# An attention block's SP queue: the third part of q sent behind the first part of k

## What is computed

```python
q = x @ w_dq.T @ w_uq.T
kv = x @ w_dkv.T @ w_ukv.T
attn = softmax(q k^T * SCALE + causal mask);  out = (attn v) @ w_out.T
h = _layernorm(x) * (1 + ca) + sa;  x = x + ga * attention(h)
h = _layernorm(x) * (1 + cb) + sb;  x = x + gb * ffn(h)
```

## Time and profile before

| | |
|---|---|
| median of 3 runs | 596.92 us (595.57 to 600.63) |
| the profiled execution | 593.84 us, span 592.1 us, granted clock 0.951 |
| busy, share of the span | PE 87%, DVE 81%, ACT 62%, POOL 53% |
| chain that ended last, by engine | PE 49%, DVE 19%, DMA 10%, issue 9%, SP's queue 5% |
| largest DMA of the chain | qs<-parts_q, 8% |
| DMA issues of the stacks | 96 to qs (median 4.0 us to landing), 96 to ks (4.7 us) |

### The profile page before, as it was taken

How to read it: one execution, slowest core, us unless ns; L and a number is a source line. 1 busy time by engine, 2 the same in 40 slices (tenths; PEclk the granted TensorE clock), 3 DMA queues, 4 the chain that set the end, 5 groups by cost and what they waited for, 6 DMA issues and landing times.

```text
span 592.1 us, 14257 instructions
## 1 busy us (share of the span) xinstructions
PE 515.4 (87%) x4912; PEld 446.2 (75%) x4912; DVE 480.8 (81%) x949; ACT 366.5 (62%) x521; POOL 311.9 (53%) x300
## 2 busy tenths in 40 slices
PE   4534685989999999999999999999999999999974
PEld 4424463788888988888888888788988898888874
DVE  3538163779999899989898989999899999887573
ACT  1524464858585866667676858585766667676320
POOL 6235232455656665755646565656665665552441
PEclk9856598899999999999999999999999999999998
DMA  8835453262707080716244351708080615210100
GB/s 246 206 46 76 50 74 75 52 95 37 128 18 145 2 161 3 121 42 90 71 68 93 50 111 31 130 7 154 0 152 13 108 39 91 55 39 2 37 19 18
DMA packets 43802, 43.74 MB, mean 74 GB/s; under 512 B 5344, under 2 KB 40800, under 8 KB 43760
## 3 DMA queue, kind: packets, MB, share of 16 engines
q1 hardware_dynamic: 43760, 43.19, 39.1%
HBM read 13.39 MB, written 4.23 MB: 30 GB/s over the span
## 4 chain that ended last, share of the span: by engine, by line
PE 49%; DVE 19%; DMA 10%; issue 9%; SPq 5%; POOL 3%; ACT 3%; DVEq 0%; POOLq 0%; ACTq 0%
DMA qs<-parts_q 8%; PE ps_s L382 6%; DVE mx L933 6%; PE ps_t L401 5%; PE ps_o L419 3%; PE ps_a L333 3%; PE ps_t L405 3%; SPq L282 3%; PE ps_a L334 3%; PE ps_a L335 3%; PE ps_c L333 3%; PE ps_c L335 2%; PE ps_c L334 2%; PE ps_o L333 2%; POOL xs L1186 2%
## 5 line engine op out<-in xcount | busy, mean ns | idle before, releaser
L794 ACT ACTIVATE score_rows<-ps_s 128x1024 f32<-128x1024 f32 x96 | 98.8, 1030 | 79.3 <-PE ps_s L382 66.2
L1246 POOL TENSOR_SCALAR_AFFINE_SELECT score_rows<-score_rows 128x512 f32<-128x512 f32 (+1 forms) x96 | 80.0, 834 | 110.4 <-ACT score_rows L794 109.8
L933 DVE TENSOR_REDUCE mx<-score_rows 128x4 f32<-128x1024 f32 (+1 forms) x96 | 114.6, 1210 | 5.7 <-POOL score_rows L1246 5.5
L806 ACT ACTIVATE p<-ps_t 128x1024 f32<-128x1024 f32 x96 | 98.5, 1026 | 17.9 <-PE ps_t L405 17.3
L382 PE MATMUL ps_s<-ks,qs 96*128 96x256 bf16 (+1 forms) x512 | 63.3, 260 | 33.2 <-DMA qs<-parts_q 29.7
L382 PEld LDWEIGHTS ps_s<-ks,qs 96*128 96x128 bf16 x512 | 37.0, 103 | 47.9 <-DMA qs<-parts_q 23.2
L1186 POOL TENSOR_TENSOR xs<-z,xs 128x512 f32<-128x512 f32 (+1 forms) x16 | 34.9, 2182 | 68.7 <-DVE z L1022 68.7
L401 PE MATMUL ps_t<-qs,ks 99*128 99x256 bf16 (+1 forms) x512 | 61.1, 254 | 11.0 <-DMA qs<-mx_rows 10.3
L401 PEld LDWEIGHTS ps_t<-qs,ks 99*128 99x128 bf16 x512 | 38.8, 101 | 17.5 <-DMA qs<-mx_rows 6.3
L405 PE MATMUL ps_t<-past_b,ident_b 128*128 128x256 bf16 (+1 forms) x192 | 46.0, 322 | 0.0
L1234 POOL TENSOR_TENSOR hid_lo<-hid,hid_hi 128x512 fp32r<-128x512 f32 x32 | 42.8, 1350 | 4.8 <-DVE hid_hi L1092 4.8
(11 more groups left out here) (166 smaller groups left out, 1631.4 us busy)
## 6 DMA issues: line engine op xcount, KB each, us to landing
qs<-parts_q SPq DMA_DIRECT2D x96, 128.0 KB, 4.0
ks<-parts_k SPq DMA_DIRECT2D x96, 128.0 KB, 4.7
xs<-x SPq DMA_DIRECT2D x16, 256.0 KB, 4.1
gates<-gates_scratch SPq DMA_DIRECT2D x16, 256.0 KB, 4.5
out<-xs SPq DMA_DIRECT2D x16, 256.0 KB, 2.9
p<-wmod SPq DMA_DIRECT2D x1, 1024.0 KB, 6.7
p<-waT SPq DMA_DIRECT2D x1, 1024.0 KB, 9.1
p<-wmod SPq DMA_DIRECT2D x1, 512.0 KB, 5.9
```

The source lines that it names most:

```text
L794: act.activation(score_rows[c % 2][:], ps_s[:], ACT.Copy).then_inc(scores_out, 1)
L806: act.activation((p0, p1)[tile][:, h0:h0 + n, :], ps_t[:].rearrange("p (h s) -> p h s", h=n), ACT.Exp, scale=SCALE).then_inc(exp_done, 1)
L933: dve.tensor_reduce(dst, score_rows[c % 2][:].rearrange("p (h k) -> p h k", h=n), AX_X, ALU.max).then_inc(max_done, 1)
L1246: pool.affine_select(out=diag, in_=diag, compare_op=ALU.is_ge, fill=NEG, base=0, pattern=[[0, n], [-1, P]], channel_multiplier=1).then_inc ...
```

## The change

SP's order within a step. The third part of q of a batch, sent before at the head of SP's next step (`stack_q(at(1), 2)`), is sent in the batch's own step, right behind the first part of k. The maxima and the gates change places, the maxima first. All DMAs, their sizes, their waits and all other engines' orders stay.

```diff
             def step(at):
-                stack_q(at(1), 2)
                 stack_q(at(0), 0)
                 stack_q(at(0), 1)
                 stack_k(at(0), 0)
+                stack_q(at(0), 2)
+                load_maxima(at(1))
                 load_gates(at(2))
-                load_maxima(at(1))
                 stack_k(at(0), 1)
                 store(at(4))
                 prefetch_x(at(-2))
```

## The result

The changed kernel takes 607.75 us (604.48 to 611.76) against 596.90 of the kernel before: ratio 1.0175, interval 1.010 to 1.025. A second comparison on another chip gave 1.0254 (1.021 to 1.030). It is slower by about 2%, outside the range of 591.5 to 601.5.

A forecast was written before the change was run, and what follows sets the result against it. Two nearly equal cycles, through the last stack DMA and through DVE and the maxima's DMA, were taken to bound the kernel. Terms 0, - 0.15 and - 0.5 summed to - 0.65 us, giving 596.2 us, range 591.5 to 601.5.

The forecast's parts named there:

- What bounds the kernel: Whole loop: PE and DVE nearly full, two nearly equal cycles, one through the last stack DMA, one through the maxima's DMA.
- Step 1: SP's queue, even loop step: q's third part is ready in its new place, 0.5 us margin (tightest 0.2), cost 0.
- Step 2: SP's queue behind the maxima: the gates' issue puts k's second part, store, x and k's third part about 0.7 us later.
- Step 3: End of the stack DMAs: k's third part, now last, lands in 3.7 us; scores start at 350.9 as before, change 0.
- Step 4: Odd loop steps, at SP's branch back: last stack DMA issued 0.3 us earlier; 0.15 us gained in all, bounds 0 to 0.35.
- Step 5: Gates' landing in the loop: later, at 348.4, but read by `gate_attn` at 350.51, so hidden with 2.1 us to spare.
- Step 6: Maxima's landing before `st_chunk` 0: taken as 0 change, bounds 0 to + 0.3 us, + 0.9 if leaving out gates gives nothing.
- The step at 85 us: Step outside the loop where SP writes clamped gates to DRAM: last stack DMA 0.5 us earlier, bounds - 1.0 to + 0.6.
- The sums: Whole kernel: - 0.65 us from 593.84 gives 593.2, the median 3.1 above it 596.2; the slower case 599.2.
- the first rival: DMA queue before `st_chunk` 0: maxima held behind q's third part, + 0.3 us in some twelve steps, 599.2 us; chance 0.15.
- far end: DMA queue before `st_chunk` 0: maxima held by the full 0.9 us a step, + 10, so 606 us; chance 0.05.
- getting shorter: Tail before the scores: k's third part lands in 3.3 us, not 3.7, - 0.4 at ten places, 592.3 us; chance 0.2.

The follow-up runs named there:

- the store and x last: Against the kernel before: store and x moved behind all stack DMAs, q's third part sent behind k's third in its own step; 593.54 us, ratio 1.0004.
- small gates: The changed kernel with the gates' DMA cut from 128 partitions to one from batch 2 on; 599.32 us, ratio 1.0114 to the kernel before.
- the swap alone: Against the kernel before: only gates and maxima change places, q's third part stays at the head of SP's next step; 628.11 us, ratio 1.0587.

## Why the prediction was wrong

- *What bounds the kernel*: right. There are two nearly equal cycles, and an earlier start of the scores is worth nothing: with PE's wait gone (the store and x last) the ratio is 1.0004. But it was used on one side alone. The same equality means that a landing that comes later can be paid for at once: PE had 0.96 us of wait before the scores but none before `st_chunk` 0.
- *Step 1, q3 ready in time*: right. In the step at 353 us SP issued q3 1.18 us before the maxima, as foretold.
- *Step 2, the gates' slot of 0.7 us*: right as an issue, k3 stands 4.44 us behind the maxima. The step left out what the issue carries. Before, the gates were issued ahead of the 1.8 us in which SP waited for the maxima (their issue ends at 340.97, the maxima's starts at 342.75), and had landed at 345.1, before the store was issued; now they lie between the maxima and k2, store, x and k3, and in the step at 353 us land at 355.75 + 4.3 = 360.1, after k3's issue at 359.11.
- *Step 3, change 0*: the step that failed first, and by the run with small gates the larger part. It took k3's landing, 3.7 us, from a row in which the gates had landed before k3 was issued, and added it to a tail that had them in. Measured 5.0 us, 4.9 and 5.2 in two other steps of the chain shown above, so the last landing came 1.3 us later and not 0.0. With the gates' bytes out it is 3.5 to 3.9 again.
- *Step 4, odd steps 0.15 earlier*: k3's issue came 4.19 us after the maxima's (391.91 - 387.72), where q3's was 4.64 after (379.08 - 374.44), so it was 0.45 earlier and not 0.3. Yet the scores began 9.29 us after the maxima's issue (397.01 - 387.72) and not 8.30 (382.74 - 374.44). Wrong in sign, for the same reason.
- *Step 5, the gates late but hidden*: right, no wait for them on DVE in the stretch.
- *Step 6, the maxima, taken at 0 with bounds to + 0.3 and + 0.9*: failed second. "Still 0.7 before `st_chunk` 0" was counted for q3's own landing, where it is the DMA behind it that `st_chunk` 0 waits for. q3's landing is in the view of its issue at 353.49 in the changed kernel:

```profile
DMA to landing us min/median/max: 4.1/4.1/4.1
```

That is 357.6, and `st_chunk` 0 starts at 358.31, 3.64 us after the maxima's issue and not 3.40. PE's own row has no wait there, but the load of its weights has:

```profile
358.31 0.45 PEld L401 LDWEIGHTS ps_t<-qs,ks 99*128 99x128 bf16 x8 [0.35 <-DMA qs<-mx_rows]
```

The step after is plainer: the maxima issued at 387.72 land at 391.84, and before that matmul PE stands idle (PE's row of that step):

```profile
391.96 0.62 PE L401 MATMUL ps_t<-qs,ks 99*128 99x128 bf16 x8 [0.68 <-DMA qs<-mx_rows]
```

So the term measures + 0.2 to + 0.8 us where it was taken at 0 (the 0.8 is at 322 us: the start of `st_chunk` 0 is 4.30 us after the maxima's issue, and 3.50 in an odd step before, 377.94 - 374.44). The Trainium skill (DMA: Bandwidth & Descriptors, Queues, rings and completion order) has an engine's semaphore write land only after all its earlier writes. In the loop the traces agree: the maxima's landing, where a trace names it, comes after q3's. But the rule is one for each engine, and the prediction read it as a bound for whole DMAs ("the maxima's signal can't come before q3's data"). In the first step with maxima it isn't one: q3, issued at 56.20, takes 6.8 us to land, until 63.0, and PE starts at 62.74 on the maxima that were issued behind it (view of q3's issue, then PE's row):

```profile
DMA to landing us min/median/max: 6.8/6.8/6.8
...
62.74 1.01 PE L401 MATMUL ps_t<-qs,ks 99*128 99x128 bf16 x8 [5.80 <-DMA qs<-mx_rows]
```

Nor does an earliest time explain the wait in the loop. q3, issued at 386.65, lands 4.2 us later, at 390.8 (view of its issue):

```profile
DMA to landing us min/median/max: 4.2/4.2/4.2
```

PE was free at 391.28 (391.96 - 0.68), and the maxima landed at 391.84, 1.0 us behind q3. By the rule alone there would be no wait, as the prediction said. That q3's bytes delay the maxima beyond it is what the run with q3 at 8 KB shows; the prediction had this as a rival and took it at 0 in the sum.

- *The step at 85 us*, - 0.5 us: k3 was issued at 93.60 and not at 94.31, 0.7 earlier, but the scores began at 99.02 and not at 98.57. Again the issue moved as forecast and the landing the other way.
- *The sums*: the first rival's 599.2 is 0.7 too low, 596.92 + 3.6 - 0.65 is 599.9; and 593.2 + 3.1 is 596.3, not 596.2. Neither matters for what failed.
- *The rivals*: the first had a right mechanism, the right sign and the right marks to look for (PE at line 401, DVE at line 1079), at a chance of 0.2 in all. That its far end (606) is near the measured 607.75 is in part luck, since the gates' bytes make up most of the loss in the loop. But it was thought of alone; the tail was only thought of as getting shorter, and the gates' bytes stood there as an argument against a gain, never as a price. How the two share the loss is only bounded. With the tail relieved (small gates) q3 in front of the maxima leaves 1.1% at most, and 0.6 us in four steps of the loop; with q3 and the gates both in front of them it is 2.4% with a shorter wait for the tail than before's; with the store and x out of the way both together cost nothing.
- *The chances*: the far end, + 0.9 us a step, was a bound of the sum and was then left out of the range; a later landing of k3 had no rival of its own.

## What to carry to other kernels

A moved DMA takes its bytes along as well as its issue: read a landing time only from a place in the queue with the same neighbours, and ask where the bytes went through before (here they had a gap behind them in which the issuing engine waited). Put what nobody waits for soon (here the store and the next input) behind what the next step waits for; in these runs the order of the rest then cost nothing (1.0004, 0.994 to 0.996, 0.992). And where two cycles are nearly equal, speeding up one gives nothing, while slowing one can cost in full (0.65 us of wait at line 401 made the step 0.7 us longer).

## What the runs showed of the hardware

- A small DMA (the maxima, 24 KB) issued 1.1 us behind one of 128 KB landed 1.0 us after it, 4.1 us after its own issue. With 1.40 us between the two issues PE did not wait for it. With 8 KB in place of the 128 KB (and the gates' 256 KB behind them), or with nothing between k1 and it as in the swap alone, PE did not wait for it in the four steps.
- One order change of two issues (the swap alone) cost 5.9%, 2.7 us a step for 0.7 us of issue that it moved; a part of it came with the clock (0.96 granted in the loop and not 1.00), with PE waiting 2.2 to 3.1 us in one piece for the stacks in each step.
